# A four-layer network on one core, scheduled by strings of letters: another order of the pieces in the repeated turn

## The chip, the core and the metric

The kernel runs on one NeuronCore of a Trainium2 chip. Five engines work side by side, each with its own stream of instructions: TensorE (PE in the profile), VectorE (DVE), ScalarE (ACT), GpSimd (POOL) and SyncE (SP, which here only issues DMAs). They meet at semaphores. The metric is the device time of one launch in microseconds (us), the median of several runs.

## What is computed

The input is 32 sequences of 256 tokens with 256 features. Four layers follow one another, each conditioned on a vector of its sequence. In short:

```python
x = L0(x)   # linear attention, 16 heads: softmax of q over features, of k over tokens
x = L1(x)   # full softmax attention, 16 heads of 16: 256 x 256 scores for each head
x = L2(x)   # two state-space scans (forward and backward), 512 channels x 16 states x 256 steps
x = L3(x)   # linear attention again, 8 heads of 32
# in L0, L1, L3:  h = silu(layernorm(y) * (1 + scale) + shift) @ W_out;  x = x + h
# in L2, for each direction:
#   delta = softplus(dlt @ Wdt + bdt);  h_t = exp(delta*A) * h_(t-1) + delta*B*u;  y = sum_n(h*C) + u*D
```

Everything is float32 but for rows of biases and masks, which are split into bfloat16 parts.

## The kernel before, in words

The 32 sequences ("batches") go through the layers in a software pipeline: while the scans of one batch run, L3 of the same batch, L1 and L0 of later batches and the lead-in of the scans of the next one run between them. The work of each layer on each engine is a Python generator that stops (`yield`) after each **piece**: a wait or two and the few instructions behind it. A letter names a generator: `L` is L0, `A` is L1 (attention), `C` the lead-in of L2 (norms, projections, softplus), `S` the scans, `P` the products of states with C, `G` the gates, `T` is L3 with the end of L2, `W` the one-time preparation of weights; on SP small letters are further strands of loads.

The order of the pieces on an engine is a string of such letters, written out in the file: `FIRST` once, then `TURN` over and over. One turn has the work of one batch of each strand, 139 pieces on DVE, 136 on ACT, 98 on PE, 55 on POOL and 21 on SP. Nothing else sets the order: an engine takes its pieces in the order of the string, and where a piece has to wait, everything behind it on that engine waits too.

```python
    running, order = set(work), chain(FIRST[engine], cycle(TURN[engine]))
    while running:
        letter = next(order)
        if letter in running and next(work[letter], "over") == "over":
```

The pieces that matter here, for one turn:

- **Scans.** 32 units, each with 4 x 256 steps in two halves. ACT computes the decay of a half into one of three PSUM banks (L699, two `exp`), POOL makes the input of a unit (L758), DVE runs the scan of a half (L714) and, in 17 of the units, multiplies the states by C (L729); in the other 15 POOL does that (L771). PE sums (L793). The PSUM bank of a half is free again once the scan, or the product, of it is done, and only then ACT may write the `exp` of the half three further on.
- **L1.** For each of eight pairs of heads PE makes scores (L375), DVE takes their maxima (L428), and the next pair's scores wait for that. Then the maxima are transposed (L381), copied by ACT (L467), put in place by a DMA, and PE makes the scores the other way round (L394), which ACT exponentiates (L471).
- **L0 and L3** are one chain each: norm statistics (L135, L138), norm on ACT (L153), transposes (L160), projections (L170), a maximum and a difference on DVE (L245, L248), k's maximum (L251), `exp` on ACT (L293, L297), v (L302), the reciprocal (L254), the block-diagonal product (L259, L261), the output (L265), norm again, POOL's product of the silu (L342), the last projection, and the sum with the input (L279). L0 of a batch shares its buffers with L3 of an earlier one, so L0's statistics follow L3's sum.
- **Lead-in of the scans.** Twice a turn DVE finishes the softplus (L572, `C_dd`), and POOL makes delta times u from it (L663) and a small memset (L665), whose result SP stores and loads again as `S_slot`. The first of these steps is called d0 below, the second d1.

Of the kernel before, what the change touches and what calls it, by code (L numbers as in the profile page):

```python
# [1458 lines left out]
def w_sp(q, K, b):  # L1459
# [3 lines left out]
    for s in range(2):  # L1463
# [16 lines left out]

FIRST = {
    "PE": (
        "WWWWWWWWWWWWWWWLLLLWLWWWWWLWWLWWWWWWWWWWWWWLWWWWWWLWWWWWWWWWWWWWLAAAAAAAAAAAAAAAAAAAAAAAAAALALLLALLLLLLAAAAAAACACACACACA"
        "ACAAAAACAAAACAACAACCLALLCLALLLLLCLSASAAAAASACSASCACSACACAACASSASASSASSACASASAACASSSACASASCSSCSSSLALSLSCLALSLSSLSSLSLCSSS"
        "LSTASAAAAASACSASCACSATC"),
    "DVE": (
        "WWWWLWWWWWWWWWWWWWWWLWLWWWWLWLWWWWWWWWWWWWWWWWWLWWWWWWWWWWWWWWLWLWWWWWWWWWWWWWWWWWWWWWWWLWAWWWAAAAAAAAAAALLLLLLLLALACCAA"
        "AAAAAACAAALLLLLLCLLASPSLPASSSCPSPSSCSPSSPASASASPASPASASPASASSPGSCPSPSSSPSPSSSSPPSSSPSPSSSSPPSSGSSAPAPSASLSPSSPSLLSSPLSPS"
        "SSLPSPGSSSPSLPC"),
    "ACT": (  # L1490
        "LLLWLLLLLLLLLLAAAAAAAAAAAAAAAAAAALLAAALALLLLLLLLLLAACAAACAACCCCCCCACCAAAACAAACAAACCALLACAALALLLLLCCCCLLLLLSSCSCSCCSASACA"
        "SSSASASCAASCSSCCSSCCSSSSCCACSCSSASSASSASSASSCASASSSASCASSSASSSACSSCSSALSLSACSASALSASLSSSLLSSLSLSCCCCSSSS"),
    "Pool": "LALCCCACSLSSSCPCCSSPSSPSSSSPSSPCSPSSSSPPSSSSSPPPSSSPSSAPSPSC",
    "SP": "LAWWALACCCACLssCCACssCSSCASCLSStSssCCACss",
}
# [12 lines left out]

ONCE = (w_pe, w_dve, w_act, w_sp)
# [163 lines left out]
```

## Time and profile before

| | |
|---|---|
| time, median of 3 runs | 4562.22 us (4561.04 to 4562.57) |
| span of the profiled execution | 4567.5 us |
| the profiled execution's own time | given by nothing but its span, which is 5.3 us above the median |
| busy: DVE, POOL, PE, ACT | 89%, 86%, 83%, 81% of the span |
| repeated stretch | 28 full turns from 568.3 to 4141.5 us |
| lead-up before it, run-out behind it | 568 us, 426 us |

A turn is counted from the start of the same piece on DVE (the product L265 of L0) in one turn to that in the next. The busy time of an engine is the time that is covered by at least one of its instructions; on DVE and ACT an instruction that doesn't wait starts some 0.09 us before the end of the one ahead of it.

### The profile page before, as it was taken

The page shows a single profiled execution, that of the slowest core. Times are in us where ns is not written, and L with a number is a line of the kernel's source. Part 1 is how long each engine was busy: PE and PEld are TensorE (multiplying, and loading weights), DVE is VectorE, ACT ScalarE, POOL GpSimd, SP SyncE. Part 2 cuts the span into 40 slices and gives each one's busy share as a digit, 9 for nine tenths or more (in the row PEclk, how much of TensorE's full clock was granted, in tenths as well). Part 3 has the DMA queues.
Part 4 walks back from the last instruction along what each step waited for, and adds up shares of the span by engine and source line. Part 5 has one row for each costly group of instructions (what it writes and reads, how often), then busy time and mean ns, then how long its engine had stood idle before and what let it go on. Part 6 is the DMA issues. An engine that isn't in the chain of part 4 may idle for free.

```text
span 4567.5 us, 73193 instructions
## 1 busy us (share of the span) xinstructions
PE 3809.5 (83%) x26068; PEld 2509.1 (55%) x26068; DVE 4075.3 (89%) x5552; ACT 3679.7 (81%) x8678; POOL 3933.3 (86%) x1836
## 2 busy tenths in 40 slices
PE   4867888888888898888888888888888889888664
PEld 3634555555555555555555555555555555555332
DVE  4312899999999999999999999999999999999985
ACT  0134788988998889888899888888899988988764
POOL 0001899999999999999999999999999999999995
PEclk7766899999999999999999999999999999999766
DMA  4002344454544444444455444444454444444441
GB/s 124 1 8 63 86 108 114 114 116 104 125 115 116 104 97 116 116 116 109 111 118 120 110 93 112 116 112 117 104 124 115 116 103 101 117 113 113 113 108 36
DMA packets 338584, 470.58 MB, mean 103 GB/s; under 512 B 56474, under 2 KB 166149, under 8 KB 338217
## 3 DMA queue, kind: packets, MB, share of 16 engines
q1 hardware_dynamic: 338218, 465.91, 43.6%
q8 instruction: 204, 3.34, 0.3%
q14 instruction: 162, 1.33, 0.1%
HBM read 378.71 MB, written 86.56 MB: 102 GB/s over the span
## 4 chain that ended last, share of the span: by engine, by line
ACT 28%; DVE 22%; POOL 21%; PE 21%; issue 6%; DMA 1%; SPq 1%; DVEq 0%; POOLq 0%; ACTq 0%
POOL S_X L758 13%; ACT ps L699 11%; PE ps L170 8%; POOL S_X L771 6%; DVE S_X L714 5%; PE ps L375 5%; DVE ps L714 5%; DVE A_sm L428 4%; DVE S_X L729 3%; PE ps L394 2%; PE ps L793 2%; PE ps L160 1%; POOL C_dd L663 1%; ACT wa L633 1%; ACT A_ring L153 1%
## 5 line engine op out<-in xcount | busy, mean ns | idle before, releaser
L758 POOL TENSOR_TENSOR S_X<-S_slot,S_bc 128x1024 f32<-128x1024 f32 x1024 | 2398.3, 2368 | 18.6 <-PE ps L793 9.4
L699 ACT ACTIVATE ps<-S_slot,acol 128x256 f32<-128x256 f32 x4096 | 1728.2, 468 | 203.3 <-DVE S_X L729 192.9
L714 DVE TENSOR_TENSOR_SCAN ps<-ps,S_X 128x512 f32<-128x512 f32 x1088 | 1301.1, 1214 | 26.2 <-ACT ps L699 16.0
L714 DVE TENSOR_TENSOR_SCAN S_X<-ps,S_X 128x512 f32<-128x512 f32 x960 | 1138.0, 1206 | 28.5 <-ACT ps L699 26.6
L771 POOL TENSOR_TENSOR S_X<-S_X,S_bc 128x1024 f32<-128x1024 f32 x480 | 1133.4, 2366 | 34.1 <-DVE S_X L714 32.0
L729 DVE TENSOR_TENSOR S_X<-ps,S_bc 128x512 f32<-128x512 f32 x1088 | 723.5, 672 | 10.4
L793 PE MATMUL ps<-S_X,sum 128*32 128x256 f32 x8192 | 621.2, 406 | 83.7 <-POOL S_X L771 73.2
L394 PE MATMUL ps<-A_qP,A_kP 32*128 32x256 f32 x2048 | 318.0, 431 | 123.8 <-ACT A_ring L471 64.1
L793 PEld LDWEIGHTS ps<-S_X,sum 128*32 128x32 f32 x8192 | 201.3, 112 | 371.4 <-issue 175.2
L428 DVE TENSOR_REDUCE A_sm<-ps 128x4 f32<-128x1024 f32 x256 | 312.2, 1220 | 91.0 <-PE ps L375 81.0
L375 PE MATMUL ps<-A_kP,A_qP 32*128 32x256 f32 x2048 | 301.3, 413 | 46.9 <-DVE A_sm L428 26.2
L394 PEld LDWEIGHTS ps<-A_qP,A_kP 32*128 32x128 f32 x2048 | 191.0, 198 | 229.4 <-ACT A_ring L471 105.5
L471 ACT ACTIVATE A_ring<-ps 128x1024 f32<-128x1024 f32 x256 | 259.0, 1012 | 49.7 <-PE ps L394 49.6
L170 PE MATMUL ps<-C_xT,wcz 128*128 128x256 f32 x1024 | 289.8, 433 | 1.0 <-ACT C_dd L609 0.9
L342 POOL TENSOR_TENSOR T_ke<-T_ke,T_xh 128x512 f32<-128x512 f32 x64 | 82.2, 1284 | 233.7 <-ACT T_xh L335 233.7
L663 POOL TENSOR_TENSOR C_dd<-C_dd 128x1024 f32<-128x1024 f32 x64 | 150.9, 2359 | 144.4 <-DVE C_dd L572 144.4
L375 PEld LDWEIGHTS ps<-A_kP,A_qP 32*128 32x128 f32 x2048 | 180.6, 190 | 164.3 <-DVE A_sm L428 91.7
L160 PE MATMUL ps<-ident,T_q 128*128 128x128 f32 x512 | 108.8, 349 | 167.5 <-ACT T_q L153 161.3
L170 PEld LDWEIGHTS ps<-C_xT,wcz 128*128 128x128 f32 x1024 | 214.1, 220 | 57.5 <-issue 24.9
L160 PEld LDWEIGHTS ps<-ident,T_q 128*128 128x128 f32 x512 | 69.4, 172 | 217.7 <-ACT T_q L153 177.3
L484 POOL TENSOR_TENSOR A_ring<-A_ring 128x512 f32<-128x512 f32 x32 | 40.9, 1279 | 170.4 <-ACT A_ring L335 170.4
L785 PE MATMUL ps<-C_xT,wD 128*128 128x256 f32 x512 | 147.7, 413 | 40.7 <-DVE S_g L741 39.8
(293 smaller groups left out, 7133.3 us busy)
## 6 DMA issues: line engine op xcount, KB each, us to landing
S_slot<-scr_dd SPq DMA_DIRECT2D x1024, 256.0 KB, 4.6
scr_dd<-C_dd SPq DMA_DIRECT2D x64, 1024.0 KB, 6.9
S_bc<-scr_bc SPq DMA_DIRECT2D x256, 256.0 KB, 6.3
L_xin<-in_x SPq DMA_DIRECT2D x32, 256.0 KB
C_mod<-scr_mod SPq DMA_DIRECT2D x32, 256.0 KB, 4.2
scr_x<-A_x SPq DMA_DIRECT2D x32, 256.0 KB, 8.5
T_x<-scr_x SPq DMA_DIRECT2D x32, 256.0 KB
out_x<-xs SPq DMA_DIRECT2D x32, 256.0 KB, 5.8
```

Of the source, the lines that this page charges most:

```text
L160: ins = p.transpose(bank[:, col * 256 + r * P:col * 256 + (r + 1) * P], src[:, r, col * P:(col + 1) * P], ident[:])
L170: ins = p.matmul(out, l, r, start=n == 0, stop=n == len(terms) - 1)
L375: ins = p.matmul(bank[o][:, t * 256:(t + 1) * 256], B["qP"][r, g, t * P:(t + 1) * P], B["kP"][r, g, :], start=True, stop=True, tile_positi ...
L394: ins = p.matmul(bank[o][:, t * 256:(t + 1) * 256], B["kP"][r, g, t * P:(t + 1) * P], B["qP"][r, g, :], start=True, stop=True, tile_positi ...
L428: v.tensor_reduce(B["sm"][:, :, 2 * n:2 * n + 2].rearrange("p t h -> p h t"), B["pair"].rearrange("p h (t m) -> p h t m", t=TT), AX, ALU.m ...
L471: a.activation(B["ring"][:, 2 * (n % 4):2 * (n % 4) + 2, :], B["pair"], ACT.Exp).then_inc(S.act.sem, 1)
L699: ins = a.activation(B["bank"][half_at(b, u, i)][:, n * T:(n + 1) * T], B["slot"][:, s, j, 0, :], ACT.Exp, scale=K.k["acol"][:, s, LINES * ...
L714: v.tensor_tensor_scan(line(x if u in ON_POOL else decay), line(decay), line(x), 0.0, ALU.mult, ALU.add).then_inc(S.scan.sem, 1)
L729: v.tensor_tensor(B["X"][:, u % RING, 2 * i:2 * i + 2, :], state, rep(B["bc"][:, s, NQ + q, :], 1, 2), ALU.mult).then_inc(S.cv.sem, 1)
L758: g.tensor_tensor(B["X"][:, u % RING], B["slot"][:, s, :, 1, :], rep(B["bc"][:, s, q, :], 1, LINES), ALU.mult).then_inc(S.b.sem, 1)
L771: g.tensor_tensor(B["X"][:, u % RING], B["X"][:, u % RING], rep(B["bc"][:, s, NQ + q, :], 1, LINES), ALU.mult).then_inc(S.cp.sem, 1)
L793: ins = p.matmul(B["sums"][32 * j:32 * j + 32, (c % 2) * T:(c % 2 + 1) * T], K.k["sum4"][:], B["X"][:, u % RING, j, :], start=False, stop= ...
```

## The change

The strings of `TURN` are replaced on all five engines. Each has the same letters as before, each as often, so every turn has the same pieces, and no wait, buffer or instruction is another. The pieces of one letter keep their order among themselves. `FIRST` has the same letters in the same order (its strings are only cut at other places). Two of the five strings:

```diff
 TURN = {
-    "PE": "ACATACASSATSASSASSTACTASASTATATCASSSATCASASCSTSCSSSLALSLSCLALSLSSLSSLSLCSSSLSTASAAAAASACSASCACSATC",
+    "PE": "ATACACAASTSSCSASATASASTASTATATCASSSSATCAASCTSCSSASLSLSSCLSSLSALSLSLSLSLCSSSLTASAAAAASCASCASSTACSAC",
...
-    "Pool": "SPSLSSSCPCCSSPSSPSSSSPSSPCSPSSSSPPSSSSSPTPPSSSPSSAPSPSC",
+    "Pool": "SPSLSSSCPCCSSPSPSSSSSSPSPSSCSPPSSPSSSPSTSPSSPSPSAPSSPSC",
```

Most pieces move by one or two places. Three places show it. In the rows below, taken from the built programs, a row is an instruction with its line, what it writes and reads, its shape and how many stand in a row; a scan is printed there as SCALAR_TENSOR_TENSOR of L714.

**POOL, from the product of unit 9's states to L3's product of the silu**, before. L663 and L665 are the step that follows d0; the last row is L3's product.

```order
L758 TENSOR_TENSOR S_X<-S_slot,S_bc 128x1024 x2
L771 TENSOR_TENSOR S_X<-S_X,S_bc 128x1024
L663 TENSOR_TENSOR C_dd<-C_dd 128x4x256
L665 MEMSET C_dd 128x4
L758 TENSOR_TENSOR S_X<-S_slot,S_bc 128x1024
L771 TENSOR_TENSOR S_X<-S_X,S_bc 128x1024
L758 TENSOR_TENSOR S_X<-S_slot,S_bc 128x1024 x4
L771 TENSOR_TENSOR S_X<-S_X,S_bc 128x1024 x2
L758 TENSOR_TENSOR S_X<-S_slot,S_bc 128x1024 x5
L771 TENSOR_TENSOR S_X<-S_X,S_bc 128x1024
L342 TENSOR_TENSOR T_ke<-T_ke,T_xh 128x512
```

The same stretch of POOL after the change, from unit 9's product on:

```order
L771 TENSOR_TENSOR S_X<-S_X,S_bc 128x1024
L758 TENSOR_TENSOR S_X<-S_slot,S_bc 128x1024 x2
L663 TENSOR_TENSOR C_dd<-C_dd 128x4x256
L665 MEMSET C_dd 128x4
L758 TENSOR_TENSOR S_X<-S_slot,S_bc 128x1024
L771 TENSOR_TENSOR S_X<-S_X,S_bc 128x1024 x2
L758 TENSOR_TENSOR S_X<-S_slot,S_bc 128x1024 x2
L771 TENSOR_TENSOR S_X<-S_X,S_bc 128x1024
L758 TENSOR_TENSOR S_X<-S_slot,S_bc 128x1024 x3
L771 TENSOR_TENSOR S_X<-S_X,S_bc 128x1024
L758 TENSOR_TENSOR S_X<-S_slot,S_bc 128x1024
L342 TENSOR_TENSOR T_ke<-T_ke,T_xh 128x512
```

Two unit inputs (L758) stand ahead of L663 now, and between L663 with its memset and L342 there are 11 of the long instructions where there were 14.

**DVE, just behind d0**, before: from the second half of unit 10 to the products of unit 14.

```order
L714 SCALAR_TENSOR_TENSOR ps<-ps,S_X 128x512
L729 TENSOR_TENSOR S_X<-ps,S_bc 128x512
L714 SCALAR_TENSOR_TENSOR S_X<-ps,S_X 128x512 x2
L714 SCALAR_TENSOR_TENSOR ps<-ps,S_X 128x512
L729 TENSOR_TENSOR S_X<-ps,S_bc 128x512
L714 SCALAR_TENSOR_TENSOR ps<-ps,S_X 128x512
L729 TENSOR_TENSOR S_X<-ps,S_bc 128x512
L254 RECIPROCAL T_kr<-T_ks 128x2
L714 SCALAR_TENSOR_TENSOR S_X<-ps,S_X 128x512 x2
L714 SCALAR_TENSOR_TENSOR ps<-ps,S_X 128x512 x2
L729 TENSOR_TENSOR S_X<-ps,S_bc 128x512 x2
```

The same stretch after the change, from the second half of unit 10 to the second half of unit 13; d0 (L572) stands in it now:

```order
L714 SCALAR_TENSOR_TENSOR ps<-ps,S_X 128x512
L572 SCALAR_TENSOR_TENSOR C_dd<-C_dd,C_tmp 128x4x256
L251 TENSOR_REDUCE T_km<-ps 128x2
L729 TENSOR_TENSOR S_X<-ps,S_bc 128x512
L714 SCALAR_TENSOR_TENSOR S_X<-ps,S_X 128x512 x2
L714 SCALAR_TENSOR_TENSOR ps<-ps,S_X 128x512 x2
L729 TENSOR_TENSOR S_X<-ps,S_bc 128x512
L254 RECIPROCAL T_kr<-T_ks 128x2
L714 SCALAR_TENSOR_TENSOR S_X<-ps,S_X 128x512
L729 TENSOR_TENSOR S_X<-ps,S_bc 128x512
L714 SCALAR_TENSOR_TENSOR S_X<-ps,S_X 128x512
```

Before, the product of a half (L729) stood three times right behind the scan that makes its input; after, something else stands between them each time.

**PE, from the transposes of the maxima (L381) to the second pair of L394**, before. L170 with L3wk is k of L3, L785 opens a sum of the scans.

```order
L793 MATMUL ps<-S_X,sum 32x256 x8
L381 MATMUL ps<-ident,A_sm 16x128 x2
L170 MATMUL ps<-T_xT,L3wk 128x256 x2
L170 MATMUL ps<-omL,bias 128x256
L170 MATMUL ps<-T_xT,L3wk 128x256 x2
L170 MATMUL ps<-omL,bias 128x256
L793 MATMUL ps<-S_X,sum 32x256 x4
L394 MATMUL ps<-A_qP,A_kP 128x256 x4
L785 MATMUL ps<-C_xT,wD 128x256 x2
L793 MATMUL ps<-S_X,sum 32x256 x4
L394 MATMUL ps<-A_qP,A_kP 128x256 x4
L793 MATMUL ps<-S_X,sum 32x256 x8
```

The same stretch of PE after the change:

```order
L381 MATMUL ps<-ident,A_sm 16x128 x2
L793 MATMUL ps<-S_X,sum 32x256 x4
L170 MATMUL ps<-T_xT,L3wk 128x256 x2
L170 MATMUL ps<-omL,bias 128x256
L170 MATMUL ps<-T_xT,L3wk 128x256 x2
L170 MATMUL ps<-omL,bias 128x256
L793 MATMUL ps<-S_X,sum 32x256 x8
L170 MATMUL ps<-C_xT,wd 96x256 x2
L785 MATMUL ps<-C_xT,wD 128x256 x2
L394 MATMUL ps<-A_qP,A_kP 128x256 x4
L793 MATMUL ps<-S_X,sum 32x256 x4
L394 MATMUL ps<-A_qP,A_kP 128x256 x4
```

Between L381 and the first L394 there are now two more sums of units, the projection L170 with wd (before, it stood behind the third L394) and L785; the two sums that stood behind the second L394 come later, so that v of L3 follows the second L394 at once.

## Rows read from the trace of the kernel before

**Rows 1.** The page: span, and busy time of each engine.

```profile
span 4567.5 us, 73193 instructions
PE 3809.5 (83%) x26068; PEld 2509.1 (55%) x26068; DVE 4075.3 (89%) x5552; ACT 3679.7 (81%) x8678; POOL 3933.3 (86%) x1836
```

**Rows 2.** Windows: stretch; us; busy PE, PEld, DVE, ACT, POOL (count); PEclk, DMA, GB/s.

```profile
1589.20:1718.30 129.10, 113.94 (x800) 75.11 (x800) 124.50 (x168) 114.62 (x272) 122.94 (x57) 0.93 0.47 110
2100.30:2227.10 126.80, 111.25 (x802) 73.76 (x800) 124.16 (x168) 114.42 (x272) 122.86 (x57) 0.96 0.48 113
568.30:4141.50 3573.20, 3136.65 (x22401) 2075.14 (x22400) 3481.95 (x4678) 3205.08 (x7589) 3440.36 (x1596) 0.95 0.48 112
```

**Rows 3.** Chain of waits, quiet turn: start us, us, what.

```profile
2160.58 2.38 POOL C_dd L663
...
2195.61 1.25 POOL T_ke L342
```

**Rows 4.** Timeline of DVE: scans with and without their product behind them.

```profile
2130.13 1.22 DVE L714 TENSOR_TENSOR_SCAN ps<-ps,S_X 128x512 f32<-128x512 f32 x1
2131.26 1.20 DVE L714 TENSOR_TENSOR_SCAN S_X<-ps,S_X 128x512 f32<-128x512 f32 x1
...
2161.01 1.22 DVE L714 TENSOR_TENSOR_SCAN ps<-ps,S_X 128x512 f32<-128x512 f32 x1
2162.27 0.69 DVE L729 TENSOR_TENSOR S_X<-ps,S_bc 128x512 f32<-128x512 f32 x1
```

**Rows 5.** Timeline of DVE: waits on other engines, quiet turn.

```profile
2133.16 1.23 DVE L428 TENSOR_REDUCE A_sm<-ps 128x4 f32<-128x1024 f32 x1
...
2138.28 1.23 DVE L428 TENSOR_REDUCE A_sm<-ps 128x4 f32<-128x1024 f32 x1 [0.30 <-PE ps L375]
...
2144.35 1.23 DVE L428 TENSOR_REDUCE A_sm<-ps 128x4 f32<-128x1024 f32 x1 [0.28 <-PE ps L375]
...
2199.15 0.69 DVE L279 TENSOR_TENSOR xs<-ps,xs 128x512 f32<-128x512 f32 x1 [0.51 <-PE ps L170]
...
2204.11 1.22 DVE L714 TENSOR_TENSOR_SCAN S_X<-ps,S_X 128x512 f32<-128x512 f32 x1 [0.17 <-ACT ps L699]
```

**Rows 6.** Timeline of POOL around d0, quiet turn.

```profile
2156.64 2.35 POOL L771 TENSOR_TENSOR S_X<-S_X,S_bc 128x1024 f32<-128x1024 f32 x1 [0.64 <-DVE S_X L714]
2160.58 2.37 POOL L663 TENSOR_TENSOR C_dd<-C_dd 128x1024 f32<-128x1024 f32 x1 [1.58 <-DVE C_dd L572]
```

**Rows 7.** Timeline of PE around the maxima, quiet turn.

```profile
2154.38 0.39 PE L381 MATMUL ps<-ident,A_sm 128*16 128x128 f32 x2 [0.41 <-DVE A_sm L428]
...
2158.88 1.13 PE L394 MATMUL ps<-A_qP,A_kP 32*128 32x256 f32 x8 [1.60 <-DMA A_qP<-A_ring]
2159.94 1.13 PE L785 MATMUL ps<-C_xT,wD 128*128 128x256 f32 x4
...
2162.65 1.07 PE L793 MATMUL ps<-S_X,sum 128*32 128x256 f32 x16
2163.65 1.13 PE L170 MATMUL ps<-L3wv,T_xT 128*128 128x256 f32 x4
...
2166.86 1.10 PE L170 MATMUL ps<-C_xT,wd 128*96 128x256 f32 x4
```

**Rows 8.** Windows, 7 us each, of a disturbed and a quiet turn.

```profile
1650.00:1657.00 7.00, 7.00 (x39) 3.52 (x40) 6.93 (x7) 5.44 (x14) 6.94 (x5) 0.52 0.69 157
2161.00:2168.00 7.00, 7.00 (x57) 4.37 (x57) 6.93 (x8) 7.00 (x17) 6.94 (x5) 1.00 0.68 150
```

**Rows 9.** Timeline of ACT, then DVE, disturbed turn: what that costs.

```profile
1657.93 0.84 ACT L302 ACTIVATE T_v<-ps,T_pc 128x256 f32<-128x256 f32 x2 [2.34 <-PE ps L170]
...
1660.83 1.22 DVE L714 TENSOR_TENSOR_SCAN S_X<-ps,S_X 128x512 f32<-128x512 f32 x1 [1.87 <-ACT ps L699]
```

**Rows 10.** Timeline of ACT, quiet turn: an attention exp, and late in the turn.

```profile
2160.53 1.00 ACT L471 ACTIVATE A_ring<-ps 128x1024 f32<-128x1024 f32 x1
...
2219.29 0.87 ACT L699 ACTIVATE ps<-S_slot,acol 128x256 f32<-128x256 f32 x2 [0.68 <-DVE S_X L729]
```

More of the change, by code:

```diff
@@ L1482 @@
     "PE": (
-        "WWWWWWWWWWWWWWWLLLLWLWWWWWLWWLWWWWWWWWWWWWWLWWWWWWLWWWWWWWWWWWWWLAAAAAAAAAAAAAAAAAAAAAAAAAALALLLALLLLLLAAAAAAACACACACACA"
-        "ACAAAAACAAAACAACAACCLALLCLALLLLLCLSASAAAAASACSASCACSACACAACASSASASSASSACASASAACASSSACASASCSSCSSSLALSLSCLALSLSSLSSLSLCSSS"
-        "LSTASAAAAASACSASCACSATC"),
+        "WWWWWWWWWWWWWWWLLLLWLWWWWWLWWLWWWWWWWWWWWWWLWWWWWWLWWWWWWWWWWWWWLAAAAAAAAAAAAAAAAAAAAAAAAAALALLLALLLLLLAAAAAAACACACA"
+        "CACAACAAAAACAAAACAACAACCLALLCLALLLLLCLSASAAAAASACSASCACSACACAACASSASASSASSACASASAACASSSACASASCSSCSSSLALSLSCLALSLSSLS"
+        "SLSLCSSSLSTASAAAAASACSASCACSATC"
+    ),
     "DVE": (
-        "WWWWLWWWWWWWWWWWWWWWLWLWWWWLWLWWWWWWWWWWWWWWWWWLWWWWWWWWWWWWWWLWLWWWWWWWWWWWWWWWWWWWWWWWLWAWWWAAAAAAAAAAALLLLLLLLALACCAA"
-        "AAAAAACAAALLLLLLCLLASPSLPASSSCPSPSSCSPSSPASASASPASPASASPASASSPGSCPSPSSSPSPSSSSPPSSSPSPSSSSPPSSGSSAPAPSASLSPSSPSLLSSPLSPS"
-        "SSLPSPGSSSPSLPC"),
+        "WWWWLWWWWWWWWWWWWWWWLWLWWWWLWLWWWWWWWWWWWWWWWWWLWWWWWWWWWWWWWWLWLWWWWWWWWWWWWWWWWWWWWWWWLWAWWWAAAAAAAAAAALLLLLLLLALA"
+        "CCAAAAAAAACAAALLLLLLCLLASPSLPASSSCPSPSSCSPSSPASASASPASPASASPASASSPGSCPSPSSSPSPSSSSPPSSSPSPSSSSPPSSGSSAPAPSASLSPSSPSL"
+        "LSSPLSPSSSLPSPGSSSPSLPC"
+    ),
     "ACT": (
-        "LLLWLLLLLLLLLLAAAAAAAAAAAAAAAAAAALLAAALALLLLLLLLLLAACAAACAACCCCCCCACCAAAACAAACAAACCALLACAALALLLLLCCCCLLLLLSSCSCSCCSASACA"
-        "SSSASASCAASCSSCCSSCCSSSSCCACSCSSASSASSASSASSCASASSSASCASSSASSSACSSCSSALSLSACSASALSASLSSSLLSSLSLSCCCCSSSS"),
+        "LLLWLLLLLLLLLLAAAAAAAAAAAAAAAAAAALLAAALALLLLLLLLLLAACAAACAACCCCCCCACCAAAACAAACAAACCALLACAALALLLLLCCCCLLLLLSSCSCSCCSA"
+        "SACASSSASASCAASCSSCCSSCCSSSSCCACSCSSASSASSASSASSCASASSSASCASSSASSSACSSCSSALSLSACSASALSASLSSSLLSSLSLSCCCCSSSS"
+    ),
     "Pool": "LALCCCACSLSSSCPCCSSPSSPSSSSPSSPCSPSSSSPPSSSSSPPPSSSPSSAPSPSC",
@@ L1497 @@
 TURN = {
-    "PE": "ACATACASSATSASSASSTACTASASTATATCASSSATCASASCSTSCSSSLALSLSCLALSLSSLSSLSLCSSSLSTASAAAAASACSASCACSATC",
+    "PE": "ATACACAASTSSCSASATASASTASTATATCASSSSATCAASCTSCSSASLSLSSCLSSLSALSLSLSLSLCSSSLTASAAAAASCASCASSTACSAC",
     "DVE": (
-        "LSLSAPSSPSPPSGPSLPASSSCPSTTTPSSCSPSSPASASASPASPASASTPATSASSPTGSCPSPSSSPSPTSSSSPPSSTSPTTSPSSSSPPSSGSSAPAPSASTLSPSSPSLLSSP"
-        "LSPSSSLPSPGSSSPSLPC"),
+        "LSLSAPSSPSPPSGPSLPACSSSTPSTPSSCTSSPSPASASAPSASPASSAPTATSAPSSSGPSCTPSSSSPTSPSSSPPSSTSPTSTSGPSSSPPSSSAPSAPSATLSSSPPSSS"
+        "LPLSSPLGSSLSPPSSSSPSLPC"
+    ),
     "ACT": (
-        "LSLLLLSSCSCSCCSASACASSSASASCAASCSSCTCSSTCCSSSSCCTACSCSSASTSASSTASSASSTCATSASSSASCTASSSTASTSSATTCSSCSSALSLSACSASALSASLSSS"
-        "LLSSLSLSCCCCSSSS"),
-    "Pool": "SPSLSSSCPCCSSPSSPSSSSPSSPCSPSSSSPPSSSSSPTPPSSSPSSAPSPSC",
-    "SP": "CSSCASCLSStSssCTCACss",
+        "LSLLLSLSCSCSCSCASACSASSASASCAASCTSCSSCSTCSCSSSCTCASCSSCSATSASSATSASSTASTSASSCSASCATSSSATSSATSTTCSSSCSALSLSSACASSSAAL"
+        "SLSCSLSLSLSLSCSCSCSS"
+    ),
+    "Pool": "SPSLSSSCPCCSSPSPSSSSSSPSPSSCSPPSSPSSSPSTSPSSPSPSAPSSPSC",
+    "SP": "SCLCSASCSCSTtSssACsCs",
 }
```

## The prediction, made before the changed kernel had run

> **What bounds the kernel now.** The page comes first: DVE is busy 89% of the span, POOL 86%, PE 83% [rows 1]. These are shares over lead-up, turns and run-out together, so the windows come next, cut at turns. A quiet turn takes 126.80 us, with DVE busy for 124.16, POOL 122.86, ACT 114.42 and PE 111.25 [rows 2]. The reader should see that DVE has 2.64 us of idle time in such a turn and POOL 3.94, and that no order of the same pieces can bring a turn far below 122 us. Why 122 and not 124.16: where DVE doesn't wait, the next instruction starts 0.09 us before the end of the one ahead (2130.13 + 1.22 = 2131.35, the next at 2131.26), and each wait loses this overlap too [rows 4]. I counted 25 such places in the turn, so waits cost 2.64 + 25 x 0.08 = 4.65 us, and a DVE that never waits would need 122.15.
>
> All 28 full turns together take 3573.2 us [rows 2], 127.61 each, 0.81 more than a quiet one: some turns are longer, as the one of 129.10. So there are two things that another order could win: waits of every turn, up to 4.65, and the disturbance, 0.81 in the mean.
>
> The chain of waits says which waits set the turn [rows 3]. It goes from d0 through POOL without a gap for 36.3 us, from L663 at 2160.58 to the end of L3's product at 2196.86; from there to PE's last projection of L3, DVE's sum, L0's norm on ACT, L0's maxima on DVE, the exps on ACT and the attention scores back to d0. Every engine has a part in it: the loop is closed by orders, not by one full engine.
>
> **The change part by part.** No instruction is added or removed, so each term is a wait.
>
> *POOL behind d0.* Before L663 POOL waits 1.58 us for d0 and before that 0.64 for a scan [rows 6]. After, two unit inputs of 2.3 us each (2.35 less the overlap) stand ahead of L663; DVE's d0 comes one scan later (1.13), and 4.6 cover 1.58 + 1.13. Between L663 and L3's product stand 11 long instructions for 14, which makes this part of the chain 3 x 2.3 = 6.9 us shorter. The chain of rows 3 is thus cut at its longest piece. What is late next is DVE itself.
>
> *DVE at L3's sum and L0's norm.* L3's sum waits 0.51, and a scan behind it 0.17 for an exp that ACT made after L0's norm [rows 5]; with the lost overlap 0.60 and 0.25. L3's product on POOL is one place earlier, and POOL gets there sooner; L3's sum and L0's statistics stand one scan (1.13) earlier on DVE. I take both waits as gone: -0.85.
>
> *Products right behind their scans.* A scan to its own product takes 2162.27 - 2161.01 = 1.26 from start to start, a scan to something else 1.13 [rows 4]: 0.13 for each pair. Counting both orders, an instruction on DVE stands right behind the one that makes its input 12 times a turn before, twice after. Three of the ten lie ahead of the first attention maximum, which comes by another way (L0's norm on ACT, L1's norm and projections, PE's scores) that I find no shorter: worth nothing. The other seven lie behind it: -0.9. The Trainium skill speaks against this term: VectorE: DVE Perf Modes, § The DRAIN you can't avoid, says that chained DVE instructions take the same time with a semaphore after each as with one at the end, which would make these pairs free and the sum smaller by 0.9. Rows 4 show a pair that is not free, though with a scan and a product, which that section doesn't measure.
>
> *The attention ladder.* Two of the eight maxima wait 0.30 and 0.28 [rows 5], three more about 0.1. The fifth's wait should go, because L3's transposes (0.6 on PE) have moved ahead out of its way, the sixth's because it stands one scan later; the second's grows by 0.3, since a sum and a projection stand between the first two scores, 0.3 more than before. Together -0.3.
>
> *What comes in.* On ACT a piece of the second softplus has moved nine places ahead, in front of six of the exps for units 27 to 29, which come 1.0 later by it. ACT idles 0.68 right there [rows 10], so 0.3 is left. L0's two maxima and its difference on DVE stand one to two places later, 1.7 in the end, with a start that is 1.13 + 0.60 = 1.7 earlier. I put 0.35 for both, seen as a wait of L0's block-diagonal product or of d1, whose product on POOL already waits.
>
> *On PE.* From L381 to the first L394 4.50 us pass, of which 1.60 is a wait for the DMA that puts the maxima in place [rows 7]. After, two sums more (1.0 by the starts of the pair of sums and of v), one projection (0.9) and L785 (1.1) stand in the 2.90 without the wait: 5.9 us. The first L394 is 1.4 late, the second 0.3, and v of L3 is 0.7 early, as two sums now follow it. The exp of the first pair stands one place (0.8) later on ACT, and started 0.5 after its scores had ended at 2160.01 [rows 10]: no term.
>
> *The disturbance.* In the long turn the clock granted in the 7 us behind that gap is 0.52, in the quiet one 1.00 [rows 8]: half and full, 1.2 and 2.4 GHz. PE had idled 1.6 us at the DMA and at several smaller places just before. The half clock makes v late, ACT waits 2.34 for it and DVE 1.87 for the exp behind [rows 9]. After, the gap of 1.6 is filled and v has 0.7 more room. I take half of the 0.81 as gone: -0.4. TensorE: Matmul & The Clock Gate, § the HAM clock gate, of the Trainium skill says that idleness brings the half clock; that agrees with the place, and no row here shows how much idleness it takes.
>
> **The sum.** -0.85 - 0.9 - 0.3 + 0.35 = -1.7 in a quiet turn (125.1), with the disturbance -2.1 in the mean turn (125.5). The 28 turns and what the run-out still has of one make 29: -61 us. The profiled execution goes from 4567.5 to 4506.5; the median lies 5.3 below, so 4501. Its own bounds: with the pairs free and the disturbance as it is, -0.8 a turn, 4539; with all eight maxima on time and no disturbance, -3.4, 4464.
>
> **The rivals.**
>
> *A, the loop is closed by other pieces just as long.* The way over L0's norm, ACT, L1's projections and the scores is full from the start of the turn (2100.30) to the first maximum (2133.16, [rows 5]), some 33 us, and I find it unchanged. If the rest is as tight, what DVE wins at one place it waits for at the next, and the turn stays within 0.3 of 126.8: 4562, the same. Against it: the part of POOL is 6.9 shorter, and the pairs cost DVE whatever else is late.
>
> *B, slower: the late first L394.* It is 1.4 late in every turn. If ACT comes to its exp without the idle time that it has now, everything behind on ACT is late by up to 0.8 there and 1.0 at units 27 to 29, and the scans wait for their exps, as the banks allow ACT to be only three halves ahead. Less the 0.9 of the pairs, that is +0.9 a turn, 4562 + 26 = 4588. It decides from where these two delays exceed the 1.7 of the sum. Against it: ACT idles 12 us a turn in all.
>
> *C, much faster: DVE nearly without waits.* If the order fits as well at the places that I didn't weigh, quiet turns take 123.2 and the disturbance is gone: -4.4 a turn, 4435. For it: ACT and PE have room. Against it: POOL is busy for 122.86 itself, the attention ladder needs a score and a maximum in turn eight times, and the first maximum keeps its date.
>
> *D, the pairs are free.* If what the seven pairs lose is made up by waits elsewhere, or isn't lost at all, the gain is 1.2 a turn, 4562 - 35 = 4527, inside the forecast's range. Rows 4 speak against it. This is how the section of VectorE: DVE Perf Modes of the Trainium skill would have it.
>
> **How the numbers follow.** Forecast 0.61, A 0.07, B 0.13, C 0.12, D 0.07. The forecast's own range is 4464 to 4539. A measurement of this kernel tells from no change what exceeds 0.2%, 9 us. Faster: 0.61 + 0.12 + 0.07 = 0.80; same 0.07; slower 0.13. The range leaves out B and the far half of C, and takes in what lies between the forecast and A: 4455 to 4560.
>
> **What would show it.** In a quiet turn of the changed kernel: 124.5 to 125.7 us long; no wait of L279 for PE above 0.2; L663 on POOL without its 1.58 at d0, and waits of L771 for scans in its place; a chain in which POOL's part is short and DVE's is longer; fewer long turns, and a wait of L394 for ACT or none in place of 1.60 for the DMA. Wrong would be: waits of L714 for ACT in quiet turns of more than 1 us together (B), waits of L428 for PE of more than 2 (A), or a half clock at a new place of the turn.

## The result, and the profile after

The changed kernel takes 4661.95 us (4660.99 to 4665.66, 4 runs) against 4561.63 (4557.94 to 4562.57, 4 runs) for the kernel before: a ratio of 1.0219 (95% interval 1.0207 to 1.0232), 100 us slower, where 61 us faster were forecast. The profiled execution has a span of 4659.3 us, 91.8 more than in [rows 1].

The page of the changed kernel, with the chain that ended last by engine:

```profile
span 4659.3 us, 73193 instructions
PE 3842.3 (82%) x26068; PEld 2516.1 (54%) x26068; DVE 4101.4 (88%) x5552; ACT 3669.0 (79%) x8678; POOL 3967.5 (85%) x1836
PE 36%; DVE 26%; ACT 21%; issue 9%; POOL 5%; DMA 1%; SPq 0%; DVEq 0%; POOLq 0%; ACTq 0%
```

The same instructions are busy for longer: DVE 26.1 us more, POOL 34.2 more, PE 32.8 more. On PE the granted clock can be the reason; DVE and POOL have no such row, so something between the engines must lengthen some of their instructions. That is the first thing to see.

Windows of the changed kernel, columns as in [rows 2]: the 28 full turns, a quiet turn, a common one and the longest kind (eight of the 28 turns take 132.9 to 134.6 us, the others 128.2 to 130.5):

```profile
561.20:4221.20 3660.00, 3175.66 (x22400) 2083.20 (x22400) 3507.93 (x4677) 3196.38 (x7593) 3473.00 (x1596) 0.94 0.47 109
2259.70:2388.00 128.30, 111.71 (x800) 73.59 (x800) 124.26 (x168) 114.01 (x272) 123.92 (x57) 0.96 0.47 111
2129.70:2259.70 130.00, 112.15 (x800) 73.90 (x800) 125.15 (x169) 114.11 (x272) 123.99 (x57) 0.95 0.47 110
1865.70:1999.80 134.10, 117.10 (x800) 75.97 (x800) 126.23 (x168) 113.61 (x270) 124.17 (x57) 0.91 0.45 106
```

A mean turn has 130.71 us, 3.10 more than before; 28 of them are 86.8 of the 91.8 us. Grouped instructions name what got longer. First the kernel before (busy us, mean ns of one; idle before them and its releasers), then the changed one:

```profile
L758 POOL TENSOR_TENSOR S_X<-S_slot,S_bc 128x1024 f32<-128x1024 f32 x1024 | 2398.3, 2368 | 18.6 <-PE ps L793 9.4 <-DMA S_slot<-scr_dd 7.7 <-issue 0.6
L663 POOL TENSOR_TENSOR C_dd<-C_dd 128x1024 f32<-128x1024 f32 x64 | 150.9, 2359 | 144.4 <-DVE C_dd L572 144.4
L572 DVE SCALAR_TENSOR_TENSOR C_dd<-C_dd,C_tmp 128x1024 f32<-128x1024 f32 x64 | 85.0, 1328 | 6.6 <-ACT C_tmp L625 3.2
```

```profile
L758 POOL TENSOR_TENSOR S_X<-S_slot,S_bc 128x1024 f32<-128x1024 f32 x1024 | 2428.2, 2389 | 90.8 <-PE ps L793 72.0 <-DMA S_slot<-scr_dd 18.1 <-issue 0.3
L663 POOL TENSOR_TENSOR C_dd<-C_dd 128x1024 f32<-128x1024 f32 x64 | 150.4, 2350 | 89.0 <-DVE C_dd L572 89.0
L572 DVE SCALAR_TENSOR_TENSOR C_dd<-C_dd,C_tmp 128x1024 f32<-128x1024 f32 x64 | 138.3, 2160 | 3.5 <-ACT C_tmp L625 3.3
```

L572 took 1.33 us in the mean and now takes 2.16: 53.3 us in all. L758 has 29.9 us more. L663's wait for L572 shrank as forecast, from 144.4 to 89.0 us, and L758 waits for PE 72.0 us instead of 9.4. The timelines of DVE and POOL show the second L572 of a turn beside POOL's unit input:

```profile
2256.66 0.63 DVE L729 TENSOR_TENSOR S_X<-ps,S_bc 128x512 f32<-128x512 f32 x1
2257.22 2.54 DVE L572 SCALAR_TENSOR_TENSOR C_dd<-C_dd,C_tmp 128x1024 f32<-128x1024 f32 x1
...
2256.29 2.38 POOL L758 TENSOR_TENSOR S_X<-S_slot,S_bc 128x1024 f32<-128x1024 f32 x1
2259.84 2.34 POOL L663 TENSOR_TENSOR C_dd<-C_dd 128x1024 f32<-128x1024 f32 x1 [1.16 <-DVE C_dd L572]
```

L758 ends at 2256.29 + 2.38 = 2258.67; L572 ends at 2259.76, 1.09 later. Nearly all of its usual 1.21 us fits behind the end of L758, though it is shown as begun 1.45 earlier. And at the first L572 of a quiet turn:

```profile
2321.76 1.21 DVE L572 SCALAR_TENSOR_TENSOR C_dd<-C_dd,C_tmp 128x1024 f32<-128x1024 f32 x1
...
2319.51 5.67 POOL L758 TENSOR_TENSOR S_X<-S_slot,S_bc 128x1024 f32<-128x1024 f32 x2
2325.13 2.36 POOL L663 TENSOR_TENSOR C_dd<-C_dd 128x1024 f32<-128x1024 f32 x1
```

Two L758 take 5.67 here, where 2 x 2.36 less the small overlap, 4.7, would do. DVE came up just as the first of them ended, ran at once, and POOL's second waited 1.0 for it. So the loss falls on one engine or the other, by who comes first. It can fall on both: where DVE comes up early in the first of the two L758, L572 is shown with up to 2.86 us and the second L758 still takes 3.3.

L572 isn't the only one. L824 also reads two tensors from SBUF, and L729 is the same operation with the same shape, but reads one of its two from PSUM (`ps`). Their groups in the changed kernel:

```profile
L729 DVE TENSOR_TENSOR S_X<-ps,S_bc 128x512 f32<-128x512 f32 x1088 | 719.4, 673 | 2.3
L824 DVE TENSOR_TENSOR xs<-T_x,T_xh 128x512 f32<-128x512 f32 x32 | 36.4, 1139 | 0.0
```

The longest of the 1088 L729 has 0.69 us, the shortest L824 0.69 and the longest 1.25, and that one ends 0.56 behind the L771 beside which it came up. So it is neither the operation nor what it writes. (In the kernel before L824 had 0.99 in the mean.)

### The profile page after: what moved, and what is told of

It reads as the page before. It is cut to its first block, busy times and chain, and to the rows that moved or that the text cites. A ratio compares the mean times of both kernels' runs of the same rounds, so it can differ in the third digit from the quotient of the medians.

```text
span 4659.3 us, 73193 instructions
## 1 busy us (share of the span) xinstructions
PE 3842.3 (82%) x26068; PEld 2516.1 (54%) x26068; DVE 4101.4 (88%) x5552; ACT 3669.0 (79%) x8678; POOL 3967.5 (85%) x1836
## 3 DMA queue, kind: packets, MB, share of 16 engines
q14 instruction: 162, 1.33, 0.1%
## 4 chain that ended last, share of the span: by engine, by line
PE 36%; DVE 26%; ACT 21%; issue 9%; POOL 5%; DMA 1%; SPq 0%; DVEq 0%; POOLq 0%; ACTq 0%
PE ps L170 21%; ACT ps L699 8%; DVE ps L714 7%; DVE S_X L714 7%; PE ps L375 4%; DVE A_sm L428 4%; ACT A_ring L471 4%; DVE S_X L729 3%; PE ps L793 3%; PE ps L394 2%; POOL S_X L758 2%; PE ps L160 2%; ACT T_q L153 1%; POOL S_X L771 1%; ACT T_ke L325 1%
## 5 line engine op out<-in xcount | busy, mean ns | idle before, releaser
L758 POOL TENSOR_TENSOR S_X<-S_slot,S_bc 128x1024 f32<-128x1024 f32 x1024 | 2428.2, 2389 | 90.8 <-PE ps L793 72.0
L714 DVE TENSOR_TENSOR_SCAN ps<-ps,S_X 128x512 f32<-128x512 f32 x1088 | 1298.9, 1213 | 41.8 <-ACT ps L699 30.2
L771 POOL TENSOR_TENSOR S_X<-S_X,S_bc 128x1024 f32<-128x1024 f32 x480 | 1133.6, 2364 | 42.0 <-DVE S_X L714 36.9
L714 DVE TENSOR_TENSOR_SCAN S_X<-ps,S_X 128x512 f32<-128x512 f32 x960 | 1137.4, 1206 | 33.9 <-ACT ps L699 31.9
L729 DVE TENSOR_TENSOR S_X<-ps,S_bc 128x512 f32<-128x512 f32 x1088 | 719.4, 673 | 2.3
L793 PE MATMUL ps<-S_X,sum 128*32 128x256 f32 x8192 | 632.1, 407 | 99.3 <-POOL S_X L771 93.6
L428 DVE TENSOR_REDUCE A_sm<-ps 128x4 f32<-128x1024 f32 x256 | 311.8, 1218 | 100.4 <-PE ps L375 98.9
L394 PE MATMUL ps<-A_qP,A_kP 32*128 32x256 f32 x2048 | 323.0, 437 | 55.1 <-ACT A_ring L471 40.1
L375 PE MATMUL ps<-A_kP,A_qP 32*128 32x256 f32 x2048 | 300.1, 411 | 29.9 <-DVE A_sm L428 27.0
L342 POOL TENSOR_TENSOR T_ke<-T_ke,T_xh 128x512 f32<-128x512 f32 x64 | 81.3, 1270 | 272.8 <-ACT T_xh L335 272.7
L394 PEld LDWEIGHTS ps<-A_qP,A_kP 32*128 32x128 f32 x2048 | 192.5, 202 | 169.9 <-ACT A_ring L471 91.5
L170 PE MATMUL ps<-C_xT,wcz 128*128 128x256 f32 x1024 | 281.0, 423 | 2.2 <-ACT C_dd L609 2.2
L170 PEld LDWEIGHTS ps<-C_xT,wcz 128*128 128x128 f32 x1024 | 203.6, 209 | 67.7 <-issue 36.8
L663 POOL TENSOR_TENSOR C_dd<-C_dd 128x1024 f32<-128x1024 f32 x64 | 150.4, 2350 | 89.0 <-DVE C_dd L572 89.0
L609 ACT ACTIVATE C_dd<-ps,bdt 128x256 f32<-128x256 f32 x256 | 106.3, 467 | 150.5 <-PE ps L538 150.4
```

The costliest lines, as they stand in the source:

```text
L170: ins = p.matmul(out, l, r, start=n == 0, stop=n == len(terms) - 1)
L375: ins = p.matmul(bank[o][:, t * 256:(t + 1) * 256], B["qP"][r, g, t * P:(t + 1) * P], B["kP"][r, g, :], start=True, stop=True, tile_positi ...
L394: ins = p.matmul(bank[o][:, t * 256:(t + 1) * 256], B["kP"][r, g, t * P:(t + 1) * P], B["qP"][r, g, :], start=True, stop=True, tile_positi ...
L428: v.tensor_reduce(B["sm"][:, :, 2 * n:2 * n + 2].rearrange("p t h -> p h t"), B["pair"].rearrange("p h (t m) -> p h t m", t=TT), AX, ALU.m ...
L714: v.tensor_tensor_scan(line(x if u in ON_POOL else decay), line(decay), line(x), 0.0, ALU.mult, ALU.add).then_inc(S.scan.sem, 1)
L729: v.tensor_tensor(B["X"][:, u % RING, 2 * i:2 * i + 2, :], state, rep(B["bc"][:, s, NQ + q, :], 1, 2), ALU.mult).then_inc(S.cv.sem, 1)
```

## The experiments

Theory P: L572, which reads two tensors from SBUF (C_dd and C_tmp), and a POOL instruction don't run together. Theory Q: PE's order is the cause. It puts sum 5 behind the transposes L381 and sum 6 behind L3's projection k, where sum 7 stood already, while DVE's gate piece (L741), which needs sum 7, has moved ahead of k's maximum (L251); so POOL's L758 and the gate piece wait for PE. Each ratio below is to the kernel before as run beside the edit (medians of 4562 to 4571 us).

### One swap in the kernel before

```diff
 POOL, from unit 9's product on:
-P C S P    (L771, L663 and L665, L758 of unit 14, L771)
+P S C P
```

> The kernel before with two neighbouring pieces swapped on POOL alone: the unit input S_b.14 (L758) now runs ahead of C_dd's product (L663), where POOL idled 1.58 us for DVE's L572. Theory P (L572, which reads two tensors from SBUF, and a POOL instruction hold each other up): the mean of the first L572 of a turn rises from 1.21 us towards 2.4, or the L758 beside it from 2.36 to over 3; L663 comes 0.7 to 2 us later and the chain over POOL makes the turn that much longer, 4580 to 4620 us. Theory Q (the order on PE alone costs the time): L572 stays at 1.21, L758 at 2.36, the turn grows by the uncovered 2.3 - 1.6 = 0.7 at most, 4562 to 4582.

Measured: 4623.24 us, ratio 1.0127 (1.0107 to 1.0146), some 59 us slower, 3 over the range of P. Timelines of DVE and POOL at that place:

```profile
2176.08 3.09 DVE L572 SCALAR_TENSOR_TENSOR C_dd<-C_dd,C_tmp 128x1024 f32<-128x1024 f32 x1
...
2175.73 2.35 POOL L758 TENSOR_TENSOR S_X<-S_slot,S_bc 128x1024 f32<-128x1024 f32 x1
2179.25 2.36 POOL L663 TENSOR_TENSOR C_dd<-C_dd 128x1024 f32<-128x1024 f32 x1 [1.16 <-DVE C_dd L572]
...
2183.95 2.35 POOL L771 TENSOR_TENSOR S_X<-S_X,S_bc 128x1024 f32<-128x1024 f32 x1 [2.18 <-DVE S_X L714]
```

L758 ends at 2178.08, L572 at 2179.17: 1.09 later again. The unit input that was to fill a gap of 1.58 us filled it and made another: DVE loses 1.9, POOL still waits 1.16 for L572 and then 2.18 for a scan that DVE's delay made late. This one swap on POOL's string costs 2.05 us a turn (3630.6 us for 28 turns against 3573.2). P holds.

### PE's and POOL's string exchanged alone

The strings are cut here at the dots; each is the whole string of the other kernel.

```diff
 the kernel before, with the changed kernel's PE string:
-"PE": "ACATACASSATSASSASST..."
+"PE": "ATACACAASTSSCSASATA..."
 the changed kernel, with this put back; and in a run of its own with
-"Pool": "SPSLSSSCPCCSSPSPSSSSSSPSPSSCSPP..."
+"Pool": "SPSLSSSCPCCSSPSSPSSSSPSSPCSPSSS..."
```

> The kernel before with only PE's turn of the changed kernel. Theory P: PE's order alone costs little, 4550 to 4580 us, L572 stays at 1.2. Theory Q (sums 5 to 7 behind L381 make POOL's S_b.13 and DVE's gate piece wait, and the half clock falls on the attention scores): 1.5 to 3.1 us a turn, 4605 to 4650, with POOL's L758 waiting for PE's L793 over 1 us in each turn.

> The changed kernel with only PE's turn of the kernel before. Theory P: the waits of L758 for L793 go, L572 stays long (1.9 and 2.4 us), and since DVE's own work is 124 us a turn not more than 1 to 1.5 us come back, 4615 to 4650. Theory Q: nearly all comes back, 4550 to 4590.

> The changed kernel with only POOL's turn of the kernel before, where one unit input less lies ahead of the first L663. Theory P: the first L572 goes back to 1.2 to 1.4 us and its L758 to 2.36, the second L572 stays at 2.4; the turn is 0.7 to 2 us shorter, 4605 to 4645. Theory Q: 4650 to 4670, as PE's order is untouched.

Measured: 4965.26 (ratio 1.0877, 1.0857 to 1.0898), 4765.61 (1.0437, 1.0415 to 1.0459) and 4778.13 us (1.046, 1.0434 to 1.0486). Both theories missed all three. In the first L572 stays at 1.26 us, so this isn't P; nor are sums 5 to 7 the main loss (the gate piece waits 15.5 us in all for them). The timelines of PE, ACT and DVE show a wait handed on:

```profile
2388.25 2.05 PE L785 MATMUL ps<-C_xT,wD 128*128 128x256 f32 x4 [8.12 <-DVE S_g L741]
2393.43 0.84 ACT L302 ACTIVATE T_v<-ps,L_pc 128x256 f32<-128x256 f32 x2 [8.93 <-PE ps L170]
2395.86 1.22 DVE L714 TENSOR_TENSOR_SCAN S_X<-ps,S_X 128x512 f32<-128x512 f32 x1 [7.75 <-ACT ps L699]
```

The new PE order has L785 of the third gate ahead of L0's v, and that fits only the new DVE order, which makes the gate earlier. The string of one engine can't be judged by giving it to the other kernel: the misfit costs more than what is looked for. The third run says one thing of use: with one unit input less ahead of the first L663, the mean of L572 is 1.73 instead of 2.16.

### Only the sums ahead, on PE

```diff
 PE, the changed kernel:
-L381, sum 5, k of L3, sums 6 and 7
+sum 5, L381, sums 6 and 7, k of L3
```

> The changed kernel with two moves on PE alone: sum 5 (L793) goes ahead of the transposes of the maxima (L381), and sums 6 and 7 go ahead of L3's projection k. If the order on PE holds back the gate piece on DVE (1.92 us of waiting for sum 7 in a turn) and POOL's L758 (1.1 for sum 5), both waits go and the turn gets 1.5 to 2.5 us shorter: 4590 to 4620 us. If these waits only stood in for time that the two-input L572 and POOL cost each other, 4650 to 4665. L572 stays at a mean of 2.1 to 2.3 in both cases.

Measured: 4622.79 us, ratio 1.0125 (1.0104 to 1.0146): 39 faster than the changed kernel, 3 above the range given. So this part of Q is real: the waits for sums fall from 56.8 to 19.9 us at the gate piece and from 72.0 to 17.2 at L758. But L572 got longer, 2.53 in the mean, outside what was expected.

### L572 with one input

This leaves out the second softplus: ACT writes the absolute value, and DVE only takes a maximum that nobody reads. The kernel no longer computes the whole result; it is a test and no candidate. Arguments are shortened to dots and the semaphore increments left out.

```diff
-v.scalar_tensor_tensor(B["dd"][:, :, 0, :], B["dd"][:, :, 0, :], 0.0, B["tmp"][:], ALU.max, ALU.add)
+v.tensor_reduce(B["most"][:], B["dd"][:, :, 0, :], AX, ALU.max)
 ...
-ins = a.activation(B["dd"][:, f, 0, :], bank[...], ACT.Identity, bias=...)
+ins = a.activation(B["dd"][:, f, 0, :], bank[...], ACT.Abs, bias=...)
```

> The changed kernel with the second softplus left out: ACT writes the absolute value instead of the sum, and in place of L572 DVE takes the maximum over the same 128x1024 elements into a buffer of 128x4, so that it reads one tensor from SBUF instead of two; nothing else changes. If two SBUF inputs are what makes L572 and POOL hold each other up, it takes 1.2 us (from 2.16), POOL's L758 beside it 2.36, and the turn loses 1.5 to 2 us: 4600 to 4625 us. If L572 is long for another reason (its tensor shared with POOL or ACT, any overlap with POOL), it stays at 1.8 or more and the time at 4650 to 4670.

> The same replacement in the kernel before, where POOL stands idle while L572 runs. By two SBUF inputs: 1.2 us as before, and 4545 to 4570 us. If the replacement is cheaper by itself, it shows here as less than 4545.

> The changed kernel with both edits, the sums ahead and L572 with one input. If the two causes are separate and together the whole loss, their gains add: 4530 to 4565 us, at or under the kernel before. If one only covered the other, no more than the better of the two alone: 4590 or more.

> The changed kernel with one input for the first L572 of a turn alone (its softplus left out, as in the run with both); the second, which in the changed kernel takes 2.4 us and after which L663 waits 1.16, keeps its two inputs. Both together gave 125 us. If the two places add in proportion to what L572 loses there (0.7 of 1.9 us on DVE, and the whole 1.0 of the L758 beside it), the first alone gives 50 to 70 us: 4590 to 4612. If the second place, which lies on the way from ACT's ln over DVE to POOL, carries the loss, the first gives under 30: 4632 or more. If the first carries it, 4535 to 4570.

Measured: 4537.37 us in the changed kernel (ratio 0.9942, 0.992 to 0.9965), 4559.34 in the kernel before (0.9983, 0.9973 to 0.9994), 4529.37 with the sums ahead too (0.9922, 0.9905 to 0.9939), and 4621.69 with the first of the two alone (1.0116, 1.0096 to 1.0136; the median of the kernel before beside it was 4570.98).

The first lies 63 us under its range, the second inside, the third just under, the fourth between two of its ranges. POOL is as busy at these places as in the changed kernel, and the same count of elements takes 1.21 us once it is read from one tensor. The edit also changes the operation and makes it write 128x4 instead of 128x1024; that neither is the reason shows in L729 and L824 above. L824 was left as it is and still takes 1.24 in the mean here. Together this decides for P. The groups in the changed kernel with one input:

```profile
L758 POOL TENSOR_TENSOR S_X<-S_slot,S_bc 128x1024 f32<-128x1024 f32 x1024 | 2399.1, 2362 | 78.6 <-PE ps L793 42.0 <-DMA S_slot<-scr_dd 35.8 <-issue 0.5
L663 POOL TENSOR_TENSOR C_dd<-C_dd 128x1024 f32<-128x1024 f32 x64 | 150.8, 2357 | 54.7 <-DVE C_most L572 54.7
L572 DVE TENSOR_REDUCE C_most<-C_dd 128x4 f32<-128x1024 f32 x64 | 77.3, 1207 | 3.5 <-ACT C_tmp L625 3.3
```

Without the two-input read the new order is 124.6 us faster than with it and 22.0 faster than the old order under the same edit; the old order gains 4 from it. The size exceeds what P was given (37 to 62). L572 lost 61.0 us, L758 29.1, and L663's wait for L572 34.3: together 124.4. That this is the time gained is luck: with the sums ahead the same three lose 84.4, 28.5 and 34.3, 147 in all, and the time falls by 93. How a microsecond lost at these places reaches the end of the turn is not shown. The first place alone gives 40 of the 125 (47 by the two ratios), under the range of "in proportion" and over that of "the second carries it", and its runs scatter from 4604.64 to 4630.65. So by subtraction the second, where L663 waits on POOL for an L572 that waits for POOL, has the larger part; it was not run alone. The two causes don't add: 125 and 39 by themselves, 133 together.

### Both L572 later on DVE

```diff
 DVE, the changed kernel:
-L572 (first), L251, L729
+L251, L729, L572 (first)
-L572 (second), L265, L714
+L265, L714, L572 (second)
```

> The changed kernel with the two L572 of a turn two pieces later on DVE (about 1.2 and 1.7 us) and nothing else: they then come up when POOL's unit input is at its end instead of 1.45 us before it. The work, the two SBUF inputs and the cover on POOL stay. If L572 waits for the POOL instruction that is under way to end, the second goes from 2.4 to 1.2 to 1.6 us, and the turn gets 1 to 2.6 us shorter: 4590 to 4630 us. If the two share bandwidth for as long as both run, L572 stays at 2 or more, as a POOL instruction runs at either place, and the time at 4655 to 4670.

> The same two moves of L572 on DVE together with the two moves of the sums on PE, with the full computation: a candidate to beat both kernels. By the wait for the instruction under way 1.2 + 1.4 us a turn come off 4623: 4545 to 4570, about the kernel before; by shared bandwidth 4615 to 4630.

Measured: 4652.34 us (ratio 1.0196, 1.0179 to 1.0213) and 4602.42 (1.0086, 1.0071 to 1.0101), against 4662 and 4623 without the move. Both lie outside what either theory gave. L572 fell to 1.81 and 1.43 us in the mean, with a POOL instruction ahead and behind as before, which speaks for waiting and against shared bandwidth. But the time was handed to POOL, as its groups with the first edit show:

```profile
L663 POOL TENSOR_TENSOR C_dd<-C_dd 128x1024 f32<-128x1024 f32 x64 | 150.2, 2347 | 161.9 <-DVE C_dd L572 161.9
L572 DVE SCALAR_TENSOR_TENSOR C_dd<-C_dd,C_tmp 128x1024 f32<-128x1024 f32 x64 | 116.0, 1812 | 2.9 <-ACT C_tmp L625 2.9
```

L663's wait grew by 72.9 us while L572 lost 22.3, so what DVE gains at a better moment, POOL pays by waiting for the result.

### The full result without L572

ACT computes the softplus as the logarithm of 1 + exp(x) by itself. Waits, semaphore increments and empty pieces are left out of the cut.

```diff
-a.activation(B["tmp"][:], B["dd"][:, :, 0, :], ACT.Abs)
-a.activation(B["tmp"][:], B["tmp"][:], ACT.Exp, scale=-1.0)
-a.activation(B["tmp"][:], B["tmp"][:], ACT.Ln, bias=1.0)
+a.activation(B["tmp"][:], B["dd"][:, :, 0, :], ACT.Exp)
+a.activation(B["dd"][:, :, 0, :], B["tmp"][:], ACT.Ln, bias=1.0)
 DVE: L572 goes; POOL: L663 waits for ACT's Ln
```

> The order with the sums ahead, and the full result without L572: ACT computes the softplus as the logarithm of 1 + exp(x), two passes of 1024 elements instead of three, straight into C_dd, and L663 on POOL waits for ACT. DVE has 2 x 1.13 us less to do in a turn. With the sums ahead and L572 at one input it took 4529; if DVE sets the turn there, 2.2 us a turn come off: 4465 to 4490. If the waits between POOL, ACT and PE set it, 4510 to 4530.

Measured: 4514.6 us, ratio 0.9877 (0.9862 to 0.9891): the fastest of all, and faster than both kernels. It gains only 15 on the 4529 of the run with the sums ahead and one input (20 by the two ratios), though DVE has two instructions of 1.2 us less a turn. The time is in the range that was given for waits between the engines; POOL's part of the chain is 21% here. (The form without the maximum would overflow for very large inputs, which these data don't have.)

## Why the prediction was wrong

**POOL behind d0** is the step that failed. "Two unit inputs of 2.3 us each ... and 4.6 cover 1.58 + 1.13" took L572 at the 1.2 us of a trace in which POOL stood idle beside it: the wait of 1.58 in [rows 6] was the time in which L572 ran alone, and so was that at d1. Filled with L758 it is no cover. L572 and L758 exclude each other, and "No instruction is added or removed, so each term is a wait" left no place for that. The mechanism moved what it was to move: the part of the chain on POOL fell to 5% (from 21%), and L663 no longer waits at d0 (0.0 in the quiet turn). None of the bounds of the sum allowed an instruction to get longer. The Trainium skill has this rule, in SBUF — State Buffer, § Who interferes with whom: a DVE instruction with two SBUF inputs contends with a GpSimd instruction that reads SBUF, and the one that comes second is blocked whole. The traces agree: L572 ends 1.09 us after L758 at two places, and costs 1.21 with one input. The forecast had no rival for it. One place goes beyond the rule, in the run-out of the changed kernel:

```profile
4405.54 7.42 DVE L572 SCALAR_TENSOR_TENSOR C_dd<-C_dd,C_tmp 128x1024 f32<-128x1024 f32 x1
...
4404.94 2.34 POOL L771 TENSOR_TENSOR S_X<-S_X,S_bc 128x1024 f32<-128x1024 f32 x1
4407.25 4.62 POOL L758 TENSOR_TENSOR S_X<-S_slot,S_bc 128x1024 f32<-128x1024 f32 x2
```

L572 came up beside L771, before either L758 had begun, and yet both L758 ran first, at full speed; L572 ended 1.09 behind the second. The kernel before has two such places behind its turns (5.20 and 3.98 us). When POOL keeps its turn and when DVE gets in between is not shown.

**The chain through it.** The chain of waits of a common turn shows L572 on the path. In the timeline this L572 is shown from 2192.96 with 1.68 us, some 0.5 more than alone, so the row "issue" of 1.44 holds both its work and its wait, and no releaser is named for either:

```profile
2187.60 2.15 PE ps L170 x8
2189.76 1.04 PE ps L793 x16
2190.80 0.03 issue
2190.83 0.48 DVE S_g L741
2191.31 0.60 DVE S_X L729
2191.91 1.14 DVE ps L714
2193.05 0.07 DVE C_dd L572
2193.12 1.44 issue
2194.56 0.69 DVE T_km L251
```

**On PE** was said to have no term, and only L394 was weighed. What came late was sum 7 behind k, for which DVE's gate piece waits (56.8 us in all, 3.5 before), and sum 5 behind L381, for which POOL's L758 waits (72.0 with the other sums, 9.4 before). The sums ahead give 39 us back. This is the second cause.

**The disturbance** did not go, but moved. PE idles 1.33 for L428 ahead of L381, and the half clock (0.66 granted over the next 5 us: part at 1.2, part at 2.4 GHz) now falls on k, which takes 3.9 us for 2.2. Timelines of PE and DVE, and the window, in the quiet turn of the changed kernel:

```profile
2313.80 0.39 PE L381 MATMUL ps<-ident,A_sm 128*16 128x128 f32 x2 [1.33 <-DVE A_sm L428]
...
2318.49 1.07 PE L793 MATMUL ps<-S_X,sum 128*32 128x256 f32 x16
...
2319.63 0.48 DVE L741 SCALAR_TENSOR_TENSOR S_g<-ps,bD,wa 128x256 f32<-128x256 f32 x1 [1.92 <-PE ps L793]
...
2314.00:2319.00 5.00, 5.00 (x32) 2.93 (x34) 3.71 (x4) 4.66 (x9) 4.13 (x2) 0.66 0.01 3
```

With one input, two neighbouring turns differ by just this. PE idles 1.33 for L428 in both, and over the next 5 us the granted clock is 1.00 in the first and 0.66 in the second:

```profile
1192.60:1317.70 125.10, 109.15 (x804) 72.20 (x800) 123.39 (x169) 114.17 (x272) 122.78 (x57) 0.97 0.49 114
1317.70:1444.30 126.60, 111.39 (x808) 73.49 (x800) 123.30 (x169) 114.08 (x272) 122.98 (x58) 0.96 0.49 112
...
1250.57 0.48 DVE L741 SCALAR_TENSOR_TENSOR S_g<-ps,bD,wa 128x256 f32<-128x256 f32 x1 [0.26 <-PE ps L793]
...
1377.20 0.48 DVE L741 SCALAR_TENSOR_TENSOR S_g<-ps,bD,wa 128x256 f32<-128x256 f32 x1 [1.90 <-PE ps L793]
```

125.10 is the 125.1 that the sum gave for a quiet turn, though in this run only 6 of the 28 are so; most lose 1.6 at the gate. With the sums ahead too, the wait went to the last L428 instead (1.39 for PE): the gate piece waits 39 us less in all, the maxima 38 more. So that edit gave 8 us and not 39 once L572 was out of the way.

**DVE at L3's sum and L0's norm** held in part: L279 has no wait in the quiet turn, but its total over the whole run is 26.8 us (28.2 before), since the longest turns have it still. **The attention ladder** gave nothing in the changed kernel, where the maxima wait 100.4 us, 91.0 before; with one input on both sides it is 73.4 against 84.8, 0.36 less for each of the 32 batches, where 0.3 was forecast. **Products right behind their scans** wasn't tried by itself, but the windows of the two kernels with one input speak for it. DVE is busy 3452.75 us in the 28 turns against 3481.99, 1.04 less a turn for the same instructions, and a product right behind its scan with a gap between them comes 1 time a turn instead of 7. So the pairs are not free, and rival D has nothing for it. The mean turn there is 126.40 against 127.64: 1.24 us less, where the sum gave 2.1; the new wait of the gate piece, 52.7 us in all against 3.9, stands against it.

**Rival B** had the side right. In 20 of the 28 turns its mechanism is absent: the scans wait 0.2 to 0.5 us for their exps. In the eight longest they wait 4.3 to 6.4, because the scores L394 are late, as B had it:

```profile
1936.49 1.02 ACT L471 ACTIVATE A_ring<-ps 128x1024 f32<-128x1024 f32 x1 [3.05 <-PE ps L394]
1939.04 1.22 DVE L714 TENSOR_TENSOR_SCAN S_X<-ps,S_X 128x512 f32<-128x512 f32 x1 [2.48 <-ACT ps L699]
1933.00:1940.00 7.00, 6.89 (x32) 3.31 (x35) 4.51 (x7) 3.26 (x8) 4.80 (x4) 0.50 0.40 150
```

What makes them late is not what B named. In all eight the first L572 takes 2.84 to 2.86 us (one turn of 128.9 has 2.85 too); in this turn k's maximum (L251) and k's exp follow it late, PE idles 1.55 for that exp at 1930, and v and the scores behind run at 0.50 of the clock. With one input no such turn is left, the longest has 128.7. Over a common turn of 129.8 the eight cost 31 us, a third of the 86.8.

What stays open is how the 86.8 us of the turns divide. The loss by L572 (125) and by the sums (39) overlap and together exceed the 100; against them stands the gain of the order itself, 22 us with one input on both sides and 30 with the sums ahead as well.

## What to carry to other kernels

Before filling an engine's idle time, ask what ran on its neighbour in that time: a duration read beside an idle engine holds only while it is idle. Look for instructions of DVE with two SBUF inputs beside POOL work, and compare the mean of the same shape before and after; the wait is booked as busy time, and in a chain it stands as time of the instruction (3.00 us in the kernel with one swap) or as "issue" behind it (1.44 here); neither names POOL. Where all orders are closed into one loop, test a theory by the smallest swap or by taking the cost away in place; a whole string of another kernel brings misfits of 100 to 400 us.

## What the runs showed of the hardware

An L572 that came up 0.35 us after the start of an L758 is shown as busy for 3.09 us, of which 1.09 lie behind L758's end. The profile counts the wait as DVE's work, so busy time rises when engines hinder each other (DVE 123.31 us a turn with one input, 125.28 with two, from 3452.75 and 3507.93 for 28 turns). The loss on POOL is smaller than on DVE: an L758 that waits takes up to 3.39 for 2.36, and the L572 that it waits for has only 1.2 us of work. After L824 the next POOL instruction (L656) takes 1.72 for 1.26. That one instruction of 1.2 us, twice in a turn of 131, could decide 125 us in 4662 was not expected.
